# A ViT layer with a mixture of experts: the mixture's 192 inputs cut as 128 and 64, and a subtraction moved to GpSimd

## The chip, the cores and the metric

The kernel runs on one NeuronCore of a Trainium2 chip. The core has TensorE (PE in the rows; its weight loads are PEld), VectorE (DVE), ScalarE (ACT), GpSimd (POOL) and SyncE (SP, here only a queue of transfers). The metric is the device time of one execution in microseconds.

## The reference

64 images of 3 x 224 x 224 become 14 x 14 patches each. A linear layer makes 192 numbers of every patch, and with a class token there are 197 tokens an image. Then come two residual steps:

```python
h = h + attention(layernorm(h))     # 12 heads of 16, q and k normalised per head
h = h + ffn(layernorm(h))           # the mixture
# ffn, for each token x of 192:
scores = sigmoid(x @ gate_weight.T)             # 8 experts in 4 groups of 2
# 2 groups by scores + bias, in them 2 experts; weights = scores, normalised
h1 = einsum('td,eid->tei', x, w1); h3 = einsum('td,eid->tei', x, w3)   # 128 inner units
y = einsum('tei,edi,te->td', silu(h1) * h3, w2, cw)
z = silu(x @ sw1.T) * (x @ sw3.T) @ sw2.T       # a shared expert
return y + z
```

All is float32 at the interface.

## The kernel before

There are a setup and two stages, each with one instruction stream per engine, which meet at semaphores.

**Split numbers.** A float32 factor is held as two float16 tiles, hi (rounded, scaled) and lo (the rest). A product of two such factors is three products on TensorE: hi by hi, hi by lo, lo by hi, added up in PSUM. 192 inputs don't fit 128 rows of the array, so they are cut into two chunks of `KC` = 96 rows (index `k`). A 192-deep product is then 2 x 3 passes.

**Setup** (L184 to L231). SyncE loads all weights and constants, ScalarE writes each `hi` (L199), VectorE each `lo` (L217). The stage ends when all engines have ended.

**Attention stage** (`phase_a`). Its `run` goes over the images with a pipeline of five steps. The first 8 images are written out, then a hardware loop takes 8 images a turn (seven turns), then come five steps that empty the pipeline. Scores (L413) are products of 32-row pieces: four heads lie at rows 0, 32, 64 and 96, and their results in four PSUM banks. Each image's result goes to DRAM by SyncE (L319, L321).

**Mixture stage** (`phase_b`). The 12608 tokens are taken in 24 groups of 512 and a last one of 320, four tokens to a partition. Three groups and the last four are written out, the others go through a loop of two groups a turn. All nine experts (the shared one is number 8) are computed for all tokens, and the unchosen ones get weight 0. For each group and expert e:

- `inner_products` (PE): 12 passes of N = 512 into two banks, `ps_h1` and `ps_h3`, two of each, L905 (hi by hi), L907, L908. It waits until the multiplication two experts back is done.
- `silu` (ACT, L971): `act1` from `ps_h1`.
- `multiply` (DVE, L1098): `inner` = `ps_h3` times `act1`. Three `inner` buffers, so it also waits for the `inlo_done` of three experts back.
- `inner_first` (ACT, L979): `in_hi`, the float16 of `inner`.
- `inner_rest` (DVE, L1104): `in_lo` = `inner` - `in_hi`.
- `outer_products` (PE, L923 to L925): 12 passes of 192 columns into two banks `ps_y`. It waits for `in_lo`, and per half for the accumulation of the expert before.
- `accumulate` (DVE, L1122; L1128 for the shared expert): adds `ps_y`, weighted, to `acc`.

The order on each engine is fixed by hand. PE in step e runs inner(e) and then outer(e-2), after step 3 the next group's transposes (L878), after step 5 its gate (L890 to L892). DVE in step e runs multiply(e), inner_rest(e-1), accumulate(e-2), and then in steps 0 and 1 the last two parts of this group's routing; for the next group, statistics in step 1 (L1004, L1008), the normalisation `bnorm` in step 2 (L1017), `yT_lo` in step 4 (L1025) and the first three routing parts in steps 6 to 8. GpSimd has only `rstds`: after the statistics an addition (L1177) and a power (L1179) give `brstd`, for which `normalise` waits. The transposes turn `bnorm` into two chunks in `ps_x`, of which ACT (L955) makes `yT_hi` and DVE `yT_lo`. SyncE loads `hin` two groups ahead and stores `acc`.

Of the kernel before, what the change touches and what calls it, by code (L numbers as in the profile page):

```python
# [103 lines left out]
def vit_layer(nc, xp, w_lin, bias_cls, w_qkv, w_proj, w_gate, gate_bias, w13, w2,  # L104
              ident, before4, before8, out):
    hidden_dram = nc.dram_tensor("hidden_dram", [IMAGES, TOKENS, C], F32).ap()
    with ExitStack() as ctx:
# [7 lines left out]
        with ExitStack():  # L115
# [8 lines left out]
            gate_hi, gate_lo = split_pair("gate", [KC, 2, EXPERTS])  # L124
            w13_hi, w13_lo = split_pair("w13", [KC, 2, NE, 2, INTER])
# [13 lines left out]
            gate_f = stage("gate_f", [KC, 2, EXPERTS])  # L139
            w13_f = stage("w13_f", [KC, 2, NE, 2, INTER])  # L140
# [98 lines left out]
def phase_a(nc, xp, hidden_dram, sem, bufs):  # L239
# [510 lines left out]
def phase_b(nc, hidden_dram, out, sem, sb, bufs):  # L750
# [6 lines left out]
    with ExitStack() as ctx:  # L757
# [111 lines left out]
        def _(pe):  # L869
            def transposes(g):  # L870
                R = rows_of(g)
                pe.wait_ge(bnorm_done, g.times(1, 1))

                if reached(g.times(1)):
                    pe.wait_ge(tanh_done, g.times(1))
                for k in range(2):
                    for t in range(T):
                        last = pe.transpose(ps_x[k][0:KC, t * R:(t + 1) * R], bnorm[0:R, t, k * KC:(k + 1) * KC],  # L878
                                            id32[0:R, 0:R])
                last.then_inc(yT_done, 1)  # L880

            def gate(g):
# [3 lines left out]
                for t in range(T):  # L886
                    s = slice(t * R, (t + 1) * R)
                    dst = ps_x[0][0:R, t * E:(t + 1) * E]
                    for k in range(2):
# [4 lines left out]

            def inner_products(g, e):
# [7 lines left out]
                for w, bank in ((0, ps_h1[b]), (1, ps_h3[b])):  # L903
                    for k in range(2):
# [92 lines left out]
        def _(dve):  # L997
# [12 lines left out]
            def normalise(g):  # L1010
# [5 lines left out]
                for t in range(T):  # L1016
                    last = dve.tensor_scalar(bnorm[0:R, t, :], hin[p][0:R, t, :], bmv[0:R, t, 0:1],  # L1017
# [83 lines left out]
            def inner_rest(g, e):  # L1101
                N, b = T * rows_of(g), e % 3
                dve.wait_ge(inhi_done, g.times(NE, e + 1))
                dve.tensor_tensor(in_lo[b][:, 0:N], inner[b][:, 0:N], in_hi[b][:, 0:N],  # L1104
                                  ALU.subtract).then_inc(inlo_done, 1)

# [33 lines left out]
            def body(g):  # L1140
                following = g.back(-1)
                for e in range(NE):
                    multiply(g, e)
                    if e > 0:
                        inner_rest(g, e - 1)
                    elif g.back(1).active():
                        inner_rest(g.back(1), NE - 1)
# [87 lines left out]
```

## Time and profile before

| | us |
|---|---|
| runs shown, median (lowest to highest, 3 runs) | 2127.14 (2127.05 to 2127.79) |
| the profiled execution, its own time | 2126.83 |
| its span, first to last instruction | 2124.9 |
| PE busy | 1922.6 (90%) |
| PE weight loads busy | 1351.2 (64%) |
| DVE busy | 1320.9 (62%) |
| ACT busy | 908.2 (43%) |
| POOL busy | 42.2 (2%) |
| mean granted TensorE clock | 0.984 |

Busy times overlap between engines, and matmuls are pipelined, so that each one's length is longer than its distance from the next. The attention stage reaches to about 1186 us, the mixture stage from there to the end. A share of busy time over the whole span mixes these two stages.

### The profile page before, as it was taken

How to read it: one execution, taken by the hardware profiler on the slowest of the kernel's cores; microseconds unless marked ns; L12 is line 12 of the kernel's file. 1: busy time of each engine (PE TensorE's matmuls, PEld its weight loads, DVE VectorE, ACT ScalarE, POOL GpSimd, SP SyncE). 2: the span in 40 equal slices, each digit the busy share in tenths (PEclk: the TensorE clock that was granted, in tenths of full speed). 3: DMA queues.
4: the chain of work that ended last, by engine and by line, in shares of the span. 5: the costliest groups of instructions: out<-in, count | busy, mean ns of one | idle time of the engine just before them, and what ended most of it. 6: DMA issues, size and time to landing. Idle time of an engine off the chain costs nothing. (4 is left out here: it accounts for less than half of the span.)

```text
span 2124.9 us, 48134 instructions
## 1 busy us (share of the span) xinstructions
PE 1922.6 (90%) x17848; PEld 1351.2 (64%) x17848; DVE 1320.9 (62%) x3554; ACT 908.2 (43%) x1878; POOL 42.2 (2%) x63
## 2 busy tenths in 40 slices
PE   3999989899899898998998699999999999999998
PEld 3777767677677776776776355555555555555556
DVE  3444444444344444444444488788888888888888
ACT  2555545455455555555555233333333333333332
POOL 0000000000000000000000000000000000000000
PEclk9999999999999999999999799999999999999999
DMA  4011111111111111111110000000000000000000
GB/s 146 16 45 44 48 43 45 46 44 45 46 45 44 46 44 46 45 45 46 44 44 10 32 16 30 17 21 23 15 30 15 22 22 15 30 15 30 16 21 13
DMA packets 31517, 74.83 MB, mean 35 GB/s; under 512 B 3435, under 2 KB 16366, under 8 KB 31214
## 3 DMA queue, kind: packets, MB, share of 16 engines
q1 hardware_dynamic: 31310, 72.10, 10.8%
q8 instruction: 126, 2.06, 0.4%
q14 instruction: 81, 0.66, 0.1%
HBM read 52.73 MB, written 19.37 MB: 34 GB/s over the span
## 5 line engine op out<-in xcount | busy, mean ns | idle before, releaser
L571 ACT ACTIVATE prob<-ps_sc 99x792 f32<-99x792 f32 x384 | 317.5, 827 | 256.0 <-PE ps_sc L413 256.0
L357 PE MATMUL ps_hid<-lin_f,xin 128*99 128x192 f32 x1536 | 289.9, 333 | 65.7 <-DVE v L684 36.1
L905 PE MATMUL ps_h<-yT_hi,w_hi 96*128 96x512 f16 (+1 forms) x900 | 342.8, 381 | 0.0
L907 PE MATMUL ps_h<-yT_lo,w_hi 96*128 96x512 f16 (+1 forms) x900 | 341.3, 379 | 0.0
L908 PE MATMUL ps_h<-yT_hi,w_lo 96*128 96x512 f16 (+1 forms) x900 | 340.9, 379 | 0.0
L357 PEld LDWEIGHTS ps_hid<-lin_f,xin 128*99 128x99 f32 x1536 | 240.3, 169 | 77.0 <-issue 47.2
L979 ACT ACTIVATE in_hi<-inner 128x512 f16<-128x512 f32 (+1 forms) x225 | 140.3, 624 | 338.3 <-DVE inner L1098 338.3
L923 PE MATMUL ps_y<-w_hi,in_hi 128*128 128x192 f16 (+1 forms) x900 | 222.4, 247 | 40.6 <-DVE acc L1122 29.0
L971 ACT ACTIVATE act<-ps_h 128x512 f32<-128x512 f32 (+1 forms) x225 | 132.3, 588 | 278.6 <-PE ps_h L908 277.9
L1122 DVE SCALAR_TENSOR_TENSOR acc<-ps_y,comb,acc 128x192 f32<-128x192 f32 (+1 forms) x700 | 242.3, 407 | 0.0
L1098 DVE SCALAR_TENSOR_TENSOR inner<-ps_h,act 128x512 f32<-128x512 f32 (+1 forms) x225 | 152.7, 679 | 130.0 <-ACT act L971 119.8
L925 PE MATMUL ps_y<-w_hi,in_lo 128*128 128x192 f16 (+1 forms) x900 | 221.2, 246 | 0.0
L924 PE MATMUL ps_y<-w_lo,in_hi 128*128 128x192 f16 (+1 forms) x900 | 221.0, 246 | 0.0
L413 PE MATMUL ps_sc<-qT,kT 32*99 32x198 f32 x3072 | 178.4, 346 | 22.1 <-issue 16.4
L428 PE MATMUL ps_o<-prob,v 98*32 98x198 f32 (+1 forms) x3072 | 171.2, 341 | 0.8 <-ACT prob L571 0.8
L908 PEld LDWEIGHTS ps_h<-yT_hi,w_lo 96*128 96x128 f16 x900 | 88.3, 98 | 106.7 <-issue 4.9
L413 PEld LDWEIGHTS ps_sc<-qT,kT 32*99 32x99 f32 x3072 | 115.4, 160 | 60.1 <-issue 36.6
L1104 DVE TENSOR_TENSOR in_lo<-inner,in_hi 128x512 f16<-128x512 f32 (+1 forms) x225 | 151.3, 672 | 0.0
L657 DVE TENSOR_REDUCE qk_var<-qk_sq 99x24 f32<-99x384 f32 x128 | 70.3, 549 | 122.8 <-ACT qk_sq L530 122.8
L923 PEld LDWEIGHTS ps_y<-w_hi,in_hi 128*128 128x128 f16 (+1 forms) x900 | 88.1, 98 | 91.4 <-DVE acc L1122 34.7
L690 DVE RECIPROCAL o_rden<-ps_mix 99x12 f32<-99x12 f32 x128 | 29.7, 232 | 187.0 <-PE ps_mix L443 159.1
L907 PEld LDWEIGHTS ps_h<-yT_lo,w_hi 96*128 96x128 f16 x900 | 89.0, 99 | 80.3 <-issue 3.2
(112 smaller groups left out, 3050.1 us busy)
## 6 DMA issues: line engine op xcount, KB each, us to landing
xin<-xp SPq DMA_DIRECT2D x64, 594.0 KB, 3.9
hidden_dram<-h SPq DMA_DIRECT2D x64, 147.0 KB
hin<-hidden_dram SPq DMA_DIRECT2D x24, 384.0 KB, 3.0
out<-acc SPq DMA_DIRECT2D x24, 384.0 KB, 2.3
w_f<-w SPq DMA_DIRECT2D x1, 1728.0 KB, 11.5
hidden_dram<-h SPq DMA_DIRECT2D x64, 0.8 KB
w_f<-w SPq DMA_DIRECT2D x1, 864.0 KB, 13.0
lin_f<-w_lin SPq DMA_DIRECT2D x1, 576.0 KB
```

The costliest lines, as they stand in the source:

```text
L357: last = pe.matmul(hid[:, t, :], xin[q][:, k, t * TR:(t + 1) * TR], lin_f[:, k, :], start=(k == 0), stop=(k == PCHUNKS - 1))
L413: last = pe.matmul(sc[:, place, m, :], kT[p][rows, quad, m * TR:(m + 1) * TR], qT[p][rows, quad, :], start=True, stop=True)
L428: last = pe.matmul(o_quad[VB * place:VB * place + VB, :], v[p][rows, m, QUAD * quad + place, :], prob[quad][rows, place, m, :], start=(m = ...
L571: act.activation(prob[quad][:, places].rearrange("p h m s -> p h (m s)"), ps_sc[0:TR, places, 0:2 * SLOTS], ACT.Exp, scale=D ** -0.5 / (SQ ...
L905: pe.matmul(bank[:, 0:N], w13_hi[:, k, e, w, :], yT_hi[p][:, k, 0:N], start=(k == 0), stop=False)
L907: pe.matmul(bank[:, 0:N], w13_hi[:, k, e, w, :], yT_lo[p][:, k, 0:N], start=False, stop=False)
L908: last = pe.matmul(bank[:, 0:N], w13_lo[:, k, e, w, :], yT_hi[p][:, k, 0:N], start=False, stop=(k == 1))
L923: pe.matmul(dst, in_hi[b][:, s], w2_hi[:, e, :], start=True, stop=False)
L924: pe.matmul(dst, in_hi[b][:, s], w2_lo[:, e, :], start=False, stop=False)
L925: last = pe.matmul(dst, in_lo[b][:, s], w2_hi[:, e, :], start=False, stop=True)
L1098: dve.scalar_tensor_tensor(out=inner[e % 3][:, 0:N], in0=ps_h3[b][:, 0:N], scalar=SA / SS, in1=act1[b][:, 0:N], op0=ALU.mult, op1=ALU.mult ...
L1122: last = dve.scalar_tensor_tensor(out=acc[p][0:R, t, :], in0=ps_y[half_no][0:R, u * C:(u + 1) * C], scalar=comb[p][0:R, t, e:e + 1], in1=b ...
```

## The change

The mixture's and the gate's input is cut as 128 and 64 instead of 96 and 96. The 64 stand twice in the rows of the second chunk: `bnorm` is 256 wide, its last 64 columns the columns 128 to 191 again, so that the transposes give 128 rows in both chunks. The weights are laid out to match by the host (`tailed`). In the second chunk of `w13_hi` rows 0 to 63 are hi and rows 64 to 127 lo of the same weights, so that one pass with `yT_hi` gives two of the three products. The third, hi by `yT_lo`, is a product of 64 rows; for w1 its weights lie in rows 0 to 63 of `w13_lo`, for w3 in rows 64 to 127, and the two are issued one after the other into different banks. `inner_rest` moves from DVE to GpSimd, where `rstds` comes before the one of expert 1. In the attention stage 16 images are written out instead of 8.

```diff
 (setup, VectorE: for w13)
+dve.scalar_tensor_tensor(out=lo[:, 0], in0=f[:, 0], scalar=SW, in1=hi[:, 0], ...)
+dve.tensor_copy(lo[0:64, 1, :, 0, :], hi[0:64, 1, :, 0, :])
+dve.tensor_copy(lo[64:128, 1, :, 1, :], hi[64:128, 1, :, 1, :]).then_inc(w_tail_done, 1)
+dve.wait_ge(w_tail_done, 1)
+dve.scalar_tensor_tensor(out=hi[64:128, 1], in0=f[64:128, 1], scalar=SW, in1=hi[64:128, 1], ...)
 (attention stage, run)
-            first = 1
+            first = 2
 (PE, transposes)
-                for k in range(2):
-                    for t in range(T):
-                        last = pe.transpose(ps_x[k][0:KC, t * R:(t + 1) * R], bnorm[0:R, t, k * KC:(k + 1) * KC],
+                for t in range(T):
+                    s = slice(t * R, (t + 1) * R)
+                    for k in range(2):
+                        last = pe.transpose(ps_x[k][:, s], bnorm[0:R, t, k * 128:(k + 1) * 128], id32[0:R, 0:R])
 (PE, gate: five products a token tile in place of six)
+                    pe.matmul(dst, yT_hi[p][:, 0, s], gate_hi[:, 0], start=True, stop=False)
+                    pe.matmul(dst, yT_hi[p][:, 0, s], gate_lo[:, 0], start=False, stop=False)
+                    pe.matmul(dst, yT_lo[p][:, 0, s], gate_hi[:, 0], start=False, stop=False)
+                    pe.matmul(dst, yT_hi[p][:, 1, s], gate_hi[:, 1], start=False, stop=False)
+                    last = pe.matmul(dst, yT_lo[p][:, 1, s], gate_lo[:, 1], start=False, stop=True)
 (PE, inner_products)
-                for w, bank in ((0, ps_h1[b]), (1, ps_h3[b])):
-                    for k in range(2):
-                        pe.matmul(bank[:, 0:N], w13_hi[:, k, e, w, :], yT_hi[p][:, k, 0:N],
-                                  start=(k == 0), stop=False)
-                        pe.matmul(bank[:, 0:N], w13_hi[:, k, e, w, :], yT_lo[p][:, k, 0:N], start=False, stop=False)
-                        last = pe.matmul(bank[:, 0:N], w13_lo[:, k, e, w, :], yT_hi[p][:, k, 0:N],
-                                         start=False, stop=(k == 1))
+                for w, bank in enumerate(banks):
+                    pe.matmul(bank, w13_hi[:, 0, e, w, :], y_hi[:, 0], start=True, stop=False)
+                    pe.matmul(bank, w13_hi[:, 0, e, w, :], y_lo[:, 0], start=False, stop=False)
+                    pe.matmul(bank, w13_lo[:, 0, e, w, :], y_hi[:, 0], start=False, stop=False)
+                    pe.matmul(bank, w13_hi[:, 1, e, w, :], y_hi[:, 1], start=False, stop=False)
+                for w, bank in enumerate(banks):
+                    rows = slice(64 * w, 64 * w + 64)
+                    last = pe.matmul(bank, w13_lo[rows, 1, e, w, :], y_lo[rows, 1], start=False, stop=True)
 (DVE, normalise, for each of four t)
-                    last = dve.tensor_scalar(bnorm[0:R, t, :], hin[p][0:R, t, :], bmv[0:R, t, 0:1],
+                    dve.tensor_scalar(bnorm[0:R, t, 0:C], hin[p][0:R, t, :], bmv[0:R, t, 0:1],
+                                      brstd[0:R, t:t + 1], ALU.subtract, ALU.mult)
+                    last = dve.tensor_scalar(bnorm[0:R, t, C:256], hin[p][0:R, t, 128:C], bmv[0:R, t, 0:1],
                                              brstd[0:R, t:t + 1], ALU.subtract, ALU.mult)
 (inner_rest and its calls are gone from DVE)
 (GpSimd)
+            def inner_rest(g, e):
+                N, b = T * rows_of(g), e % 3
+                pool.wait_ge(inhi_done, g.times(NE, e + 1))
+                settle(pool, settled)
+                pool.tensor_tensor(in_lo[b][:, 0:N], inner[b][:, 0:N], in_hi[b][:, 0:N],
+                                   ALU.subtract).then_inc(inlo_done, 1)
             def body(g):
-                if g.back(-1).active():
-                    rstds(g.back(-1))
+                for e in range(NE):
+                    if e == 1 and g.back(-1).active():
+                        rstds(g.back(-1))
+                    inner_rest(g, e)
```

## Rows read from the trace of the kernel before

**Rows 1.** The page, section 2: busy tenths in 40 slices of the span.
```profile
PE   3999989899899898998998699999999999999998
...
DVE  3444444444344444444444488788888888888888
```

**Rows 2.** Stretches of the mixture stage: start:end us, length, busy us (instructions), TensorE clock.
```profile
2036.20:2072.40 36.20, 34.47 (x252) 20.53 (x251) 31.20 (x89) 11.99 (x22) 1.79 (x2) 1.00 0.03 12
...
1420.65:1458.30 37.65, 35.61 (x247) 21.05 (x245) 30.68 (x87) 12.09 (x21) 1.26 (x2) 0.95 0.06 21
```

**Rows 3.** Timeline of one expert: start us, us, engine, line, what [idle before].
```profile
1603.49 0.38 PE L905 MATMUL ps_h<-yT_hi,w_hi 96*128 96x512 f16 x1
...
1606.08 0.25 PE L923 MATMUL ps_y<-w_hi,in_hi 128*128 128x192 f16 x1
...
1606.91 0.69 DVE L1098 SCALAR_TENSOR_TENSOR inner<-ps_h,act 128x512 f32<-128x512 f32 x1 [0.47 <-ACT act L971]
...
1607.07 0.38 PE L905 MATMUL ps_h<-yT_hi,w_hi 96*128 96x512 f16 x1
...
1607.52 0.68 DVE L1104 TENSOR_TENSOR in_lo<-inner,in_hi 128x512 f16<-128x512 f32 x1
1607.71 0.63 ACT L979 ACTIVATE in_hi<-inner 128x512 f16<-128x512 f32 x1 [0.84 <-DVE inner L1098]
...
1608.12 1.39 DVE L1122 SCALAR_TENSOR_TENSOR acc<-ps_y,comb,acc 128x192 f32<-128x192 f32 x4
```

**Rows 4.** Timeline of VectorE alone, one group: four of its L1098.
```profile
1660.88 0.69 DVE L1098 SCALAR_TENSOR_TENSOR inner<-ps_h,act 128x512 f32<-128x512 f32 x1
...
1669.02 0.69 DVE L1098 SCALAR_TENSOR_TENSOR inner<-ps_h,act 128x512 f32<-128x512 f32 x1 [1.89 <-ACT act L971]
...
1684.39 0.69 DVE L1098 SCALAR_TENSOR_TENSOR inner<-ps_h,act 128x512 f32<-128x512 f32 x1 [0.20 <-DVE rank L1059]
...
1697.87 0.66 DVE L1098 SCALAR_TENSOR_TENSOR inner<-ps_h,act 128x512 f32<-128x512 f32 x1
```

**Rows 5.** Timeline around the normalisation of the group that begins in rows 4.
```profile
1661.40 1.04 POOL L1179 TENSOR_TENSOR brstd<-bvareps,minus_half 128x4 f32<-128x4 f32 x1
...
1663.39 1.24 DVE L1017 TENSOR_SCALAR bnorm<-hin,bmv,brstd 128x192 f32<-128x192 f32 x4
...
1664.69 1.08 PE L878 MATMUL ps_x<-id,bnorm 128*96 128x128 f32 x8 [0.49 <-DVE bnorm L1017]
...
1665.60 0.38 PE L905 MATMUL ps_h<-yT_hi,w_hi 96*128 96x512 f16 x1
```

**Rows 6.** Timeline of the attention stage where 32-row score products begin and end.
```profile
1154.80 0.25 PE L342 MATMUL ps_mix<-proj_hi,onT_lo 96*99 96x192 f16 x1
...
1154.97 0.93 PE L413 MATMUL ps_sc<-qT,kT 32*99 32x198 f32 x16
...
1155.83 0.88 PE L428 MATMUL ps_o<-prob,v 98*32 98x198 f32 x16
```

**Rows 7.** The page, section 5: the score products by line and shape, whole span.
```profile
L413 PE MATMUL ps_sc<-qT,kT 32*99 32x198 f32 x3072 | 178.4, 346 | 22.1 <-issue 16.4
```

**Rows 8.** Groups of GpSimd alone, by shape, whole span.
```profile
L1179 POOL TENSOR_TENSOR brstd<-bvareps,minus_half 128x4 f32<-128x4 f32 x24 | 31.7, 1321 | 2.0
L1177 POOL TENSOR_SCALAR bvareps<-bmv 128x4 f32<-128x4 f32 x24 | 5.5, 228 | 1990.7 <-DVE bmv L1008 1990.7
...
L226 POOL MEMSET qk_norm<- 99x768 f32 x2 | 1.4, 737 | 0.0
```

**Rows 9.** SyncE's timeline of image stores, on both sides of one loop edge.
```profile
263.72 0.34 SPq L319 DMA_DIRECT2D hidden_dram<-h  x1
...
287.67 0.33 SPq L319 DMA_DIRECT2D hidden_dram<-h  x1
...
305.02 0.34 SPq L319 DMA_DIRECT2D hidden_dram<-h  x1
```

**Rows 10.** Timeline of the setup: VectorE's last conversion of weights.
```profile
17.75 6.82 DVE L217 SCALAR_TENSOR_TENSOR w_lo<-w_f,w_hi 96x4608 f16<-96x4608 f32 x2 [6.01 <-ACT w_hi L199]
```

More of the change, by code:

```diff
@@ L123, in vit_layer @@
             proj_hi, proj_lo = split_pair("proj", [KC, 2, C])
-            gate_hi, gate_lo = split_pair("gate", [KC, 2, EXPERTS])
-            w13_hi, w13_lo = split_pair("w13", [KC, 2, NE, 2, INTER])
+            gate_hi, gate_lo = split_pair("gate", [128, 2, EXPERTS])
+            w13_hi, w13_lo = split_pair("w13", [128, 2, NE, 2, INTER])
             w2_hi, w2_lo = split_pair("w2", [INTER, NE, C])
@@ L138, in vit_layer @@
             proj_f = stage("proj_f", [KC, 2, C])
-            gate_f = stage("gate_f", [KC, 2, EXPERTS])
-            w13_f = stage("w13_f", [KC, 2, NE, 2, INTER])
+            gate_f = stage("gate_f", [128, 2, EXPERTS])
+            w13_f = stage("w13_f", [128, 2, NE, 2, INTER])
             w2_f = stage("w2_f", [INTER, NE, C])
@@ L767, in phase_b @@
         brstd = sb("brstd", [128, T])
-        bnorm = sb("bnorm", [128, T, C])
-        yT_hi = [sb(f"yT_hi{p}", [KC, 2, GT], F16) for p in range(2)]
-        yT_lo = [sb(f"yT_lo{p}", [KC, 2, GT], F16) for p in range(2)]
+        bnorm = sb("bnorm", [128, T, 256])
+        yT_hi = [sb(f"yT_hi{p}", [128, 2, GT], F16) for p in range(2)]
+        yT_lo = [sb(f"yT_lo{p}", [128, 2, GT], F16) for p in range(2)]
         act1 = [sb(f"act1{p}", [INTER, GT]) for p in range(2)]
@@ L902, in inner_products @@
                     pe.wait_ge(mul_done, g.times(NE, e - 1))
-                for w, bank in ((0, ps_h1[b]), (1, ps_h3[b])):
-                    for k in range(2):
-                        pe.matmul(bank[:, 0:N], w13_hi[:, k, e, w, :], yT_hi[p][:, k, 0:N],
-                                  start=(k == 0), stop=False)
-                        pe.matmul(bank[:, 0:N], w13_hi[:, k, e, w, :], yT_lo[p][:, k, 0:N], start=False, stop=False)
-                        last = pe.matmul(bank[:, 0:N], w13_lo[:, k, e, w, :], yT_hi[p][:, k, 0:N],
-                                         start=False, stop=(k == 1))
+                banks = (ps_h1[b][:, 0:N], ps_h3[b][:, 0:N])
+                y_hi, y_lo = yT_hi[p][:, :, 0:N], yT_lo[p][:, :, 0:N]
+                for w, bank in enumerate(banks):
[6 more added lines that the diff above has]
+                    last = pe.matmul(bank, w13_lo[rows, 1, e, w, :], y_lo[rows, 1], start=False, stop=True)
                 last.then_inc(inner_done, 1)
@@ L1024, in yT_out @@
                     dve.wait_ge(yThi_done, g.times(2, k + 1))
-                    dve.scalar_tensor_tensor(out=yT_lo[p][:, k, 0:N], in0=ps_x[k][0:KC, 0:N], scalar=SX,
+                    dve.scalar_tensor_tensor(out=yT_lo[p][:, k, 0:N], in0=ps_x[k][:, 0:N], scalar=SX,
                                              in1=yT_hi[p][:, k, 0:N], op0=ALU.mult,
@@ L1099, in multiply @@
                                          in1=act1[b][:, 0:N], op0=ALU.mult, op1=ALU.mult).then_inc(mul_done, 1)
[L1101 to L1105, printed above, removed]
             def accumulate(g, e):
@@ L1143, in body @@
                     multiply(g, e)
[L1144 to L1147, printed above, removed]
                     if e > 1:
@@ L1213 @@
     w2 = np.concatenate([np.asarray(L0_ffn_w2), np.asarray(L0_ffn_sw2)[None]])
-    w13 = np.stack([w1, w3], 1).reshape(NE, 2, INTER, 2, KC).transpose(4, 3, 0, 1, 2)
+    w13 = tailed(np.stack([w1, w3], 1).reshape(NE * 2 * INTER, C)).reshape(128, 2, NE, 2, INTER)
     gate_bias = np.empty((128, LANES, EXPERTS), np.float32)
```

33 lines of the change are left out of this document (24 added, 9 removed).

## The prediction

> **What bounds the kernel now.** I read the page's slices first. From slice 23 on, the mixture stage, PE reads 9 and VectorE (DVE) 8 in nearly every slice [rows 1]. Two engines are almost full, and a cut on one alone would soon meet the other. The stretches of one group's length say the same: of 36.20 us in the unrolled tail PE is busy 34.47 and DVE 31.20. In the loop 17 stretches of 37.65 follow each other, and five of them read a clock of 0.95, which is about 3.8 us at 1.2 GHz instead of 2.4 in each [rows 2].
>
> Then one expert in order of time. PE takes 2.59 us for the twelve inner products (1603.49 to 1606.08, 0.2155 each) and 0.99 for the outer ones, 3.58 together. The multiplication on DVE starts 3.42 us after the first inner product (2.59 plus 0.83 of pipeline end and Silu). On DVE inner, in_lo and the four acc follow 0.61, 0.60 and 1.30 us apart, 2.51 in all [rows 3]. DVE has more to do in some experts: routing in 0, 1, 6, 7, 8, statistics in 1, normalisation in 2, yT_lo in 4. Write D2 for the start of expert 2's multiplication. DVE's starts are D2 = 1660.88, D4 = 8.14 later, D8 another 15.37 later, and the next D2 13.48 after that, 36.99 in all [rows 4]. So who sets the end changes within a group:
> - D8 to D2: three steps of 4.49 against PE's 3.58. DVE binds, and PE waits for acc.
> - D2 to D4: a chain. Normalisation (starts D2+2.51, takes 1.24), transposes on PE, inner products of expert 4 from D2+4.72 [rows 5], then 3.42 to D4. 4.72 + 3.42 = 8.14.
> - D4 to D8: four PE steps of 3.58 plus the gate and a little of DVE, 15.37. PE binds.
>
> **The change, part by part.**
>
> *Nine passes.* Per expert eight 128-row products and two 64-row ones on different rows and banks. If the two run side by side, that is 9 x 0.2155 = 1.94 us. The attention stage shows that they can: 16 passes on 32-row pieces take 0.93 us, of which the last one's own length is 0.35 [rows 7], so 0.04 apart where a 192-column f16 pass alone has 0.08. It also shows what the change of piece costs. L342 to the first L413 is 0.17 us against the usual 0.08, so 0.09 going in. Coming out, the last L413 starts near 1155.55 and L428 at 1155.83; 0.28 less 0.155 for its share of four is 0.12 [rows 6]. I take 0.21 for both, so I = 2.15 us an expert. The bounds: 1.94 (both hidden) and 2.40 (no overlap, ten passes, 2.155, plus 0.24).
>
> The Trainium skill speaks against this part (TensorEngine Tiling (Array Packing), Key Properties): going from one tiling to another, not merely to another tile, drains TensorE. The gaps at L413 agree in direction. The page gives no price, so the sum keeps the rows' 0.21; with nothing for it, it would be rival 1's.
>
> *inner_rest from DVE to GpSimd.* On its new engine it issues a wait, a semaphore increment and the subtraction, no DMA; nothing of SyncE's queue is passed. It takes 0.60 us of DVE per expert [rows 3]. No GpSimd subtraction of 128x512 is in the trace. Its memset of 768 elements takes 0.737 and a 4-element operation 0.228 [rows 8], so a stream costs about 0.83 ns an element. One stream of 512 gives 0.65 us, two (both inputs one after the other) 1.08, three 1.51. I take 1.15, next to two; the lower bound is 0.5, and for the upper one I double it to 2.4. The Trainium skill (GPSIMD Engine Reference, section 3.1) has 4497 ns for a two-input add of 2048 elements, some 1.1 us for 512 by proportion; the sum is the same by it.
>
> Usually this hides. in_hi starts 0.80 after inner and takes 0.63 [rows 3], so in_lo would be there about D+2.8, and PE asks for it two inner products later, D+4.5 or more. The exception is expert 1. GpSimd now runs rstds before inner_rest(1), and rstds waits for DVE's statistics, which end at D2. The power starts at D2+0.52 and takes 1.04 in this group [rows 5], 1.32 in the mean [rows 8]: it ends at D2+1.84. Then 0.1 of wait, 1.15 of subtraction and 0.1 to PE: outer products of expert 1 at D2+3.2. Behind that wait on PE stand the outer products (0.99), the transposes, and inner(4). The transposes take 0.91 now [rows 5]; with 128 columns in place of 96 I take 1.1. PE reaches inner(4) at D2 + 3.2 + 0.99 + 1.1 = 5.3, against 4.72 now.
>
> *Normalisation.* Four more DVE operations of 64 columns. The present four take 1.16 from start to start, 0.29 each; at a third of the width I take 0.15, so 0.6 us (bounds 0.3, 1.16). DVE then finishes at D2+3.7, before the outer products of expert 1 end at 4.19, so GpSimd's delay covers it. Without that delay it is what is late: D2+3.85 for the transposes.
>
> *One group after.* D2 to D4: 5.3 + 2.15 + 0.83 = 8.3 (was 8.14). D4 to D8: 15.37 less 4 x 0.44 for PE, less 0.1 for the gate's four fewer products and 0.1 for DVE's in expert 7: 13.4. D8 to D2: DVE loses 3 x 0.60, 13.48 - 1.80 = 11.7. Sum 33.4, which is 3.6 less. For 24 full groups: -86 us. The last group of 320 columns, smaller and with no next group: -2. The first normalisation stands free: +0.6.
>
> *TensorE's clock.* Now PE stands in pieces of about 1 us around experts 1 to 3. Afterwards it has inner(3) done near D2+0.2 and waits to D2+3.2, in one piece. Five of 17 stretches now lose about 1.9 us of PE time [rows 2], though part of that falls where PE waits anyway. I expect half of the 24 groups to gain such an episode at 1.2 us: +14 (bounds 0 and +35).
>
> *Attention, loop from image 16.* Stores lie 17.35 us apart, at the loop edge 23.95 [rows 9]. There are six such edges, and they cost between 2.8 and 6.6 us more, 27.4 together. The first images, unrolled, run at the same 17.3. One edge goes: -4.6.
>
> *Setup.* The stage ends with DVE's conversions, 6.82 us for 6336 elements, 1.08 ns each [rows 10]. After: the same elements, two copies of 1152 (0.6 to 2.5 us), a wait in between, and w13's transfer a third larger ahead of them. I take +3.5 (0.6 to 6.3). Gate pieces are too small to count.
>
> **Sum.** The profiled execution took 2126.83 us (span 2124.9 and 1.9 around it), 0.3 under the median of 2127.14, so no correction. 2126.8 - 86 - 2 + 0.6 + 14 - 4.6 + 3.5 = 2052 us.
>
> **Rivals.**
> 1. *The 64-row pair costs nothing beyond its pass.* I = 1.94: expert 4 comes 0.21 earlier, D4 to D8 0.7 shorter (DVE's routing in 7 takes a little back). Group 32.4, 1.0 less in each of 24: 2052 - 24 = 2028, and 2014 if the clock doesn't fall more often. For it: loads of weights run ahead of the products everywhere in this trace. Against: the gaps at L413 [rows 6].
> 2. *The pair runs as two passes, or draining costs more.* I = 2.40, group 34.6: 2052 + 30 = 2082. For it: no 64-row piece is in the trace. Together with a subtraction of 2 us, 2102.
> 3. *It ends on the other side: GpSimd becomes the bound.* With P for one subtraction a group needs 9 P + 1.6 us there (the power and its addition, [rows 8]), and no work of another engine can pass it, since outer products and, three experts on, the multiplication wait for in_lo. The loop's groups now take 36.99 [rows 4] to 37.65, about 37.3, which it equals at P = 3.97. At P = 4.5 a group takes 42.1, 24 x 4.8 = +115: 2240 us. For it: a power of 4 elements takes 1.32 us there, so its time there isn't set by width alone. Against: the memset's rate, from which 3.97 is more than twice three streams.
> 4. *DVE doesn't get shorter*, because GpSimd's traffic slows its operations by what it was relieved of. A power takes 1.04 us in one group and 1.32 in the mean [rows 5, 8], so something is shared beside DVE's work. D8 to D2 then stays 13.48: +43, 2095.
>
> **Chances and range.** The forecast with its own terms (2035 to 2070) 0.45; rival 1 0.22; rival 2 0.15; rival 3 0.06; rival 4 0.07; a mixture that is 0.2% or less from before 0.02; the rest below 2010, 0.03. The range 2010 to 2100 holds the first cases. About 0.2% (4 us) is what a measurement can tell from no change. Faster by more 0.91, same 0.02, slower 0.07 (rival 3 and a sliver of 4).
>
> **What would show it.** Inner products of one expert span 2.15 us from the first to the outer products' first, 1.94 by rival 1, 2.4 by rival 2. GpSimd's subtractions read near 1.15 us, busy about 290 us in total. Steps from D8 to D2 shrink to 11.7. The longest PE wait in each group ends with GpSimd's in_lo ahead of expert 1's outer products, about 3 us. The clock reads 0.95 in more than half of the stretches. Five loop edges are left in the attention stage and the image distance stays 17.35. The forecast is wrong if groups stay above 36 us, or if PE waits for in_lo in experts other than 1.

## The result, and the profile after

The changed kernel takes 2147.07 us (median of 4 runs, 2145.86 to 2147.82) against 2127.1: ratio 1.0096, interval 1.008 to 1.0112. The forecast was 2052 us with a range from 2010 to 2100. It is slower where faster was forecast. The profiled span is 2146.0 us, 21.1 longer than before, and its granted clock 0.957 instead of 0.984.

The page's slices, which answer [rows 1], show PE and DVE both lower than before in the mixture stage, and GpSimd (POOL) at 2 to 3. Neither of the two is nearly full any more.

```profile
PE   3999999899899998998998688888888798897888
...
DVE  3444444444444444444443587887878878788787
...
POOL 0000000000000000000000123333233322333332
```

Two stretches of the mixture stage (start:end, length, then busy us of PE, weight loads, DVE, ACT and POOL with instructions, the TensorE clock, DMA share, GB/s), against [rows 2]: PE is busy 31 to 32 us where it was 35.6, at a clock of 0.91 and 0.95.

```profile
1383.00:1420.65 37.65, 31.37 (x219) 17.80 (x218) 29.23 (x79) 11.25 (x20) 10.91 (x11) 0.91 0.06 21
1600.00:1638.33 38.33, 32.05 (x226) 17.87 (x225) 30.61 (x83) 11.88 (x21) 11.61 (x11) 0.95 0.06 21
```

The inner products of one expert [rows 3], from its first to the first outer product: 2.14 us (1605.59 to 1607.73), forecast 2.15. The two 64-row products run as a pair, one row for both. The distances from start to start on its two sides are 0.31 and 0.32 against the usual 0.2155; together that is the price of the piece change, 0.20.

```profile
1605.59 0.38 PE L929 MATMUL ps_h<-yT_hi,w_hi 128*128 128x512 f16 x1
...
1607.41 0.10 PEld L936 LDWEIGHTS ps_h<-yT_lo,w_lo 64*128 64x128 f16 x2 [0.42 <-issue]
...
1607.73 0.26 PE L950 MATMUL ps_y<-w_hi,in_hi 128*128 128x192 f16 x1
```

VectorE's four multiplications of one group [rows 4]. D4, D8, D2 and the next D4 here: D4 to D8 14.18, D8 to D2 13.15, D2 to D4 10.91 (forecast 13.4, 11.7, 8.3).

```profile
1605.33 0.69 DVE L1127 SCALAR_TENSOR_TENSOR inner<-ps_h,act 128x512 f32<-128x512 f32 x1 [4.14 <-ACT act L998]
...
1619.51 0.69 DVE L1127 SCALAR_TENSOR_TENSOR inner<-ps_h,act 128x512 f32<-128x512 f32 x1 [0.20 <-DVE rank L1088]
...
1632.66 0.68 DVE L1127 SCALAR_TENSOR_TENSOR inner<-ps_h,act 128x512 f32<-128x512 f32 x1
...
1643.57 0.69 DVE L1127 SCALAR_TENSOR_TENSOR inner<-ps_h,act 128x512 f32<-128x512 f32 x1 [3.53 <-ACT act L998]
```

Around that group's normalisation [rows 5], D2 = 1632.66. PE waits for GpSimd's in_lo(1) until 1635.55, D2+2.9 (forecast 3.2). But the normalisation, which began at D2+1.9, is over only near D2+5.4, and PE starts inner(4) at D2+7.4 instead of 5.3. Look at two rows: a 192-column operation of DVE of 0.98 us, where the next one takes 0.37, and a 64-column one of 1.15, where the others take 0.30. They end 0.05 to 0.12 us after GpSimd's two subtractions do. And the first products of expert 4 read 0.63 us each instead of 0.38: TensorE is at 1.2 GHz.

```profile
1633.26 1.04 POOL L1197 TENSOR_TENSOR brstd<-bvareps,minus_half 128x4 f32<-128x4 f32 x1
...
1634.26 2.28 POOL L1203 TENSOR_TENSOR in_lo<-inner,in_hi 128x512 f16<-128x512 f32 x2
1634.56 0.98 DVE L1044 TENSOR_SCALAR bnorm<-hin,bmv,brstd 128x192 f32<-128x192 f32 x1
...
1635.45 1.15 DVE L1046 TENSOR_SCALAR bnorm<-hin,bmv,brstd 128x64 f32<-128x64 f32 x1
...
1635.55 0.25 PE L950 MATMUL ps_y<-w_hi,in_hi 128*128 128x192 f16 x1 [2.54 <-POOL in_lo L1203]
...
1636.52 0.37 DVE L1044 TENSOR_SCALAR bnorm<-hin,bmv,brstd 128x192 f32<-128x192 f32 x1
...
1638.27 1.96 PE L901 MATMUL ps_x<-id,bnorm 128*128 128x128 f32 x8 [1.56 <-DVE bnorm L1046]
...
1640.03 0.63 PE L929 MATMUL ps_h<-yT_hi,w_hi 128*128 128x512 f16 x1
```

By shape over the mixture stage (line, engine, operation, names, shapes, count, busy us, mean ns, idle before), first after, then before:

```profile
L1044 DVE TENSOR_SCALAR bnorm<-hin,bmv,brstd 128x192 f32<-128x192 f32 x92 | 48.1, 523 | 0.0
L1046 DVE TENSOR_SCALAR bnorm<-hin,bmv,brstd 128x64 f32<-128x64 f32 x92 | 47.1, 512 | 0.0
...
L1079 DVE TENSOR_TENSOR cmp<-masked 128x256 f32<-128x256 f32 x24 | 26.3, 1095 | 0.0
...
L1079 DVE TENSOR_TENSOR cmp<-gsum 128x64 f32<-128x64 f32 x24 | 20.9, 869 | 0.0
L1093 DVE TENSOR_SCALAR score<-half 128x32 f32<-128x32 f32 x24 | 20.7, 861 | 1.1 <-ACT half L989 1.1
L1100 DVE TENSOR_SCALAR chosen<-rank 128x16 f32<-128x16 f32 x24 | 20.2, 841 | 0.0
```

```profile
L1017 DVE TENSOR_SCALAR bnorm<-hin,bmv,brstd 128x192 f32<-128x192 f32 x92 | 28.5, 372 | 0.0
...
L1050 DVE TENSOR_TENSOR cmp<-masked 128x256 f32<-128x256 f32 x24 | 9.9, 414 | 0.0
...
L1050 DVE TENSOR_TENSOR cmp<-gsum 128x64 f32<-128x64 f32 x24 | 5.1, 214 | 0.0
...
L1064 DVE TENSOR_SCALAR score<-half 128x32 f32<-128x32 f32 x24 | 4.1, 171 | 1.2 <-ACT half L962 1.2
...
L1071 DVE TENSOR_SCALAR chosen<-rank 128x16 f32<-128x16 f32 x24 | 3.9, 163 | 0.0
```

So the chosen, score and comparison operations (parts of the routing) got 0.66 to 0.69 us longer each with the same operands; inner (687 ns) and acc (407 ns), one input of which is in PSUM, did not change by a nanosecond. GpSimd's side [rows 8]: a subtraction takes 1.159 us, forecast 1.15.

```profile
L1203 POOL TENSOR_TENSOR in_lo<-inner,in_hi 128x512 f16<-128x512 f32 x211 | 243.5, 1159 | 473.7 <-ACT in_hi L1006 473.7
L1197 POOL TENSOR_TENSOR brstd<-bvareps,minus_half 128x4 f32<-128x4 f32 x23 | 23.9, 1037 | 1.9
```

The rest of the forecast: the stores of images, the first and the last [rows 9], and the setup's conversions [rows 10]. Five loop edges are left of six, as forecast (24.05, 20.36, 22.16, 24.03, 21.93 us).

```profile
93.17 0.37 SPq L341 DMA_DIRECT2D hidden_dram<-h  x1
...
1185.78 0.32 SPq L341 DMA_DIRECT2D hidden_dram<-h  x1
```

```profile
21.93 1.96 DVE L239 SCALAR_TENSOR_TENSOR w_lo<-w_f,w_hi 128x1728 f16<-128x1728 f32 x1
```

The last store was at 1185.49 before, so everything ahead of the mixture stage cost +0.3 us (forecast -1.1). The conversions end at 23.9, earlier than the 24.6 of before [rows 10]. The loss is all in the mixture stage.

Below, "group" is the mean distance from one group's D2 to the next over groups 3 to 21. The three parts are means that leave out the first of these, so they don't always add up to it. "Low clock" is the number and total length of the episodes at 1.2 GHz that begin between 1206 us (about where the mixture's first multiplication stands) and 2130 us. The one that is left in e6 and in e8 to e13 begins behind the last multiplication.

| kernel | us | ratio to before [interval] | group | D2-D4 | D4-D8 | D8-D2 | low clock |
|---|---|---|---|---|---|---|---|
| before | 2127.1 | | 37.32 | 8.71 | 15.37 | 13.30 | 7, 22 us |
| after | 2147.1 | 1.0096 [1.008, 1.0112] | 38.33 | 11.23 | 14.19 | 12.95 | 24, 133 us |
| e1_vector | 2129.6 | 1.0018 [1.0006, 1.0029] | 37.54 | 9.90 | 14.47 | 13.26 | 15, 82 us |
| e2_only_pool | 2143.4 | 1.0085 [1.0067, 1.0103] | 37.63 | 9.32 | 15.30 | 12.89 | 11, 44 us |
| e3_rstds_later | 2143.7 | 1.0084 [1.0061, 1.0106] | 38.30 | 10.57 | 14.20 | 13.60 | 24, 120 us |
| e4_fill | 2103.5 | 0.9892 [0.9874, 0.991] | 36.47 | 9.38 | 14.19 | 12.95 | 2, 7 us |
| e5_probe | 2207.8 | 1.0371 [1.0348, 1.0394] | 40.94 | 13.10 | 14.53 | 13.35 | 23, 154 us |
| e6_before_fill | 2120.0 | 0.9965 [0.9952, 0.9979] | 36.80 | 8.16 | 15.37 | 13.30 | 1, 4 us |
| e7_tail_scalar | 2087.3 | 0.9806 [0.9784, 0.9828] | 35.82 | 8.14 | 14.47 | 13.27 | 8, 27 us |
| e8_tail_fill | 2083.7 | 0.979 [0.9768, 0.9811] | 35.66 | 7.96 | 14.46 | 13.26 | 1, 1 us |
| e9_mixed | 2042.1 | 0.9593 [0.9577, 0.9609] | 33.85 | 8.07 | 13.12 | 12.68 | 1, 1 us |
| e10_three | 2073.5 | 0.9736 [0.972, 0.9752] | 35.14 | 8.07 | 13.81 | 13.29 | 1, 2 us |
| e11_pool_tail_fill | 2082.3 | 0.9785 [0.9768, 0.9802] | 35.59 | 8.49 | 14.24 | 12.91 | 1, 1 us |
| e12_order_only | 2082.2 | 0.9776 [0.9751, 0.9802] | 35.56 | 7.97 | 14.33 | 13.29 | 1, 3 us |
| e13_mixed_no_order | 2068.5 | 0.972 [0.9691, 0.9749] | 35.12 | 8.07 | 14.29 | 12.81 | 1, 2 us |

### The profile page after: what moved, and what is told of

It is laid out like the page before. It is cut to its first block and busy times, and to the rows that moved or that the text cites. A ratio compares the mean times of both kernels' runs of the same rounds, so it can differ in the third digit from the quotient of the medians.

```text
span 2146.0 us, 47266 instructions
## 1 busy us (share of the span) xinstructions
PE 1866.3 (87%) x17298; PEld 1298.9 (61%) x17298; DVE 1316.4 (61%) x3435; ACT 905.4 (42%) x1878; POOL 290.7 (14%) x288
## 5 line engine op out<-in xcount | busy, mean ns | idle before, releaser
L1203 POOL TENSOR_TENSOR in_lo<-inner,in_hi 128x512 f16<-128x512 f32 (+1 forms) x225 | 256.4, 1144 | 503.8 <-ACT in_hi L1006 503.8
L950 PE MATMUL ps_y<-w_hi,in_hi 128*128 128x192 f16 (+1 forms) x900 | 229.3, 255 | 106.5 <-POOL in_lo L1203 60.5
L951 PE MATMUL ps_y<-w_lo,in_hi 128*128 128x192 f16 (+1 forms) x900 | 226.9, 252 | 0.0
L952 PE MATMUL ps_y<-w_hi,in_lo 128*128 128x192 f16 (+1 forms) x900 | 226.8, 252 | 0.0
L1195 POOL TENSOR_SCALAR bvareps<-bmv 128x4 f32<-128x4 f32 (+1 forms) x25 | 5.7, 228 | 1343.4 <-DVE bmv L1035 1343.4
L929 PE MATMUL ps_h<-yT_hi,w_hi 128*128 128x512 f16 (+1 forms) x450 | 178.6, 397 | 0.0
L930 PE MATMUL ps_h<-yT_lo,w_hi 128*128 128x512 f16 (+1 forms) x450 | 177.7, 395 | 0.0
L931 PE MATMUL ps_h<-yT_hi,w_lo 128*128 128x512 f16 (+1 forms) x450 | 175.9, 391 | 0.0
L932 PE MATMUL ps_h<-yT_hi,w_hi 128*128 128x512 f16 (+1 forms) x450 | 174.3, 387 | 0.0
## 6 DMA issues: line engine op xcount, KB each, us to landing
w_f<-w SPq DMA_DIRECT2D x1, 864.0 KB, 11.3
```

The costliest lines, as they stand in the source:

```text
L929: pe.matmul(bank, w13_hi[:, 0, e, w, :], y_hi[:, 0], start=True, stop=False)
L930: pe.matmul(bank, w13_hi[:, 0, e, w, :], y_lo[:, 0], start=False, stop=False)
L931: pe.matmul(bank, w13_lo[:, 0, e, w, :], y_hi[:, 0], start=False, stop=False)
L932: pe.matmul(bank, w13_hi[:, 1, e, w, :], y_hi[:, 1], start=False, stop=False)
L950: pe.matmul(dst, in_hi[b][:, s], w2_hi[:, e, :], start=True, stop=False)
L951: pe.matmul(dst, in_hi[b][:, s], w2_lo[:, e, :], start=False, stop=False)
```

## The experiments

**e1 and e2: the two halves alone.** e1 is the changed kernel with in_lo back on VectorE; e2 is the kernel before with in_lo on GpSimd and nothing else.

```diff
# e1: after, the subtraction back on VectorE (e2: before, the same edit the other way).
# Shortened: the function and its calls move with the line.
-                pool.tensor_tensor(in_lo[b][:, 0:N], inner[b][:, 0:N], in_hi[b][:, 0:N],
+                dve.tensor_tensor(in_lo[b][:, 0:N], inner[b][:, 0:N], in_hi[b][:, 0:N],
                                   ALU.subtract).then_inc(inlo_done, 1)
```

> The kernel after the change with inner_rest put back on VectorE, in its old place; nine passes, 128/64 and the attention loop stay. Theory 1 (VectorE instructions that read or write SBUF through both ports wait for a running GpSimd subtraction): every long one of the kernel after (score 861 ns, chosen 841, first cmp 869 and 1095, bnorm 523 and 512) falls back to before's 171, 163, 214, 414, 372 and about 300; D8 to D2 13.1 to 13.5 us, D2 to D4 about 8.7, group about 35.5, 2080 us. Theory 2 (only the late in_lo of expert 1 and the lowered clock cost time): the same direction, but the long VectorE instructions should not change by this.

> The kernel before with inner_rest alone moved to GpSimd (96/96, twelve passes). Theory 1: VectorE gets back what it was relieved of (D8 to D2 stays near 13.1), D2 to D4 near 11.3 by the late in_lo of expert 1; group 39.6, 2182 us. Theory 2: D8 to D2 falls to 11.7, group 38.2, 2149 us.

Measured: 1.0018 and 1.0085. Moving in_lo to GpSimd alone makes the kernel 0.85% slower, and nine passes with their four 64-column operations give nothing. Both expectations missed in part. In e1 the long operations fell back as theory 1 had it, but the kernel came out at 2129.6 and not at 2080: the 64-column operations and the clock, which e7 and e8 price, weren't in it. e2's 2143 us is near theory 2's 2149, but not by its way: D8 to D2 is 12.89 and not 11.7, and D2 to D4 is 9.32 where theory 1 had 11.3. In e2 the same operations are longer as in after (score 861 ns, chosen 841, the 256-wide comparison 1095), with twelve passes and no 64-column operations there: it is GpSimd's subtraction that does it, not the new shapes.

What GpSimd did to VectorE's steps can be added up. Step e reaches from expert e's multiplication to the next one (means of the loop). The table takes DVE's steps in e1, subtracts the 0.60 of in_lo that goes, adds the extra time of that step's operations from the rows above (for the 64-column bnorm against e1's 306 ns), and compares with after:

| step | e1 | -0.60, plus the wait of | gives | after |
|---|---|---|---|---|
| 0 | 4.84 | comparison 128x256, 0.68 | 4.92 | 4.96 |
| 1 | 4.69 | none | 4.09 | 4.08 |
| 2 | 4.52 | four bnorm at 523 for 372 ns, four at 512 for 306, 1.43 | 5.35 | 5.39 |
| 6 | 3.32 | score, 0.69 | 3.41 | 3.43 |
| 7 | 3.83 | comparison 128x64, 0.66 | 3.89 | 3.95 |
| 8 | 3.75 | chosen, 0.68 | 3.83 | 3.90 |

Of 5.4 us that VectorE is relieved of in a group, 4.1 come back as waits. Steps 3 to 5 have few such operations: step 4 keeps the relief (3.71 to 3.15), step 5 doesn't change (3.61 to 3.65), and step 3 (5.37 to 5.84) is set by TensorE and its clock (3.98 in e4, where the clock is held).

**e3: GpSimd's order.** The one wait that I had forecast, rstds ahead of inner_rest(1), is taken away.

```diff
-                    if e == 1 and g.back(-1).active():
+                    if e == 2 and g.back(-1).active():
                         rstds(g.back(-1))
```

> The kernel after with one line changed: rstds stands before inner_rest(2) instead of before inner_rest(1), so no subtraction waits behind the statistics. Theory 2: the wait of about 2.5 us before expert 1's outer products goes, the clock stays up, group 34.3, about 2065 us. Theory 1: that wait goes too, but D8 to D2 stays at 13.1 or more and bnorm still collides; group about 36, 2090 to 2100 us.

Measured: 2143.7; the interval of its ratio holds after's 1.0096, and both theories had expected a gain of about 50 us or more. D2-D4 loses 0.66 and D8-D2 gains 0.65: the wait moves. That it was long in after (24 waits, 60.5 us in all, below) doesn't make it worth anything.

```profile
PE ps_y L950 <- POOL in_lo L1203: 60.5, 24, 2.9
```

The trace of e3 shows where it moved to. Without the power ahead of it, the subtraction of expert 1 starts already in step 1. So one operation of the normalisation meets a subtraction where two did, but the routing in step 1 meets one too (4.08 to 4.73 us). There an operation on 4 columns takes 0.82 us, 0.17 in e1. The reduction ahead of it, with one input in SBUF as well, runs wholly beside the subtraction and keeps its 0.19 (means 187 and 186 ns in e3 and e1):

```profile
1586.55 1.16 POOL L1203 TENSOR_TENSOR in_lo<-inner,in_hi 128x512 f16<-128x512 f32 x1 [3.80 <-ACT in_hi L1006]
1586.69 0.19 DVE L1114 TENSOR_REDUCE den<-wsel 128x4 f32<-128x32 f32 x1
1586.91 0.82 DVE L1115 TENSOR_SCALAR den<-den 128x4 f32<-128x4 f32 x1
```

**e4: the clock.** Eleven idle products of 512 columns, whose result nobody reads, fill TensorE's wait in step 3.

```diff
+                    if e == 3 and following.active():
+                        p = g.mod(2)
+                        for _ in range(11):
+                            pe.matmul(ps_x[1][:], w13_hi[:, 0, e, 0, :], yT_hi[p][:, 0, :], start=True, stop=True)
```

> The kernel after with 11 idle products of 512 columns (2.4 us) on TensorE between inner products and outer products of expert 3, into a bank that nobody reads then; they fill the wait for in_lo, so only the clock can change. If the half clock after that wait is on the path (6.8 us of it per group in 13 of 24): clock near 1.0 in the mixture stage and 2 us a group less, 2100 us. If it is not: 2147 within 5 us.

Measured: 2103.5, 43.6 us less than after, with 2 episodes at 1.2 GHz instead of 24. D4-D8 and D8-D2 are the same to 0.01, D2-D4 is 1.85 shorter. D2 to D4 in a group of after, then in one of e4: 10.91 at 0.84, 9.34 at 1.00.

```profile
1632.66:1643.57 10.91, 6.80 (x42) 4.38 (x42) 7.38 (x21) 3.43 (x6) 4.67 (x5) 0.84 0.12 36
```

```profile
1572.64:1581.98 9.34, 7.79 (x53) 4.42 (x53) 7.38 (x20) 3.31 (x6) 4.68 (x5) 1.00 0.13 42
```

So idle work makes the kernel faster, because it stands where TensorE waits anyway and what follows then runs at 2.4 GHz.

**e5: a probe.** e1, with one more GpSimd subtraction per expert on buffers of its own. No engine waits for its result.

```diff
+                for e in range(NE):
...
+                    pool.wait_ge(inhi_done, g.times(NE, e + 1))
...
+                    pool.tensor_tensor(probe[:, 0:N], probe_in[:, 0:N], probe_in[:, 0:N], ALU.subtract).then_inc(probed, 1)
```

> e1_vector (inner_rest on VectorE) with an extra GpSimd subtraction of 128x512 on tiles of its own, at the moments at which the kernel after runs its own; nobody waits for it. So only a shared resource can slow the rest. Theory 1 (VectorE's instructions with both SBUF ports wait for it): score, chosen, the first cmp and the first bnorm grow by 0.5 to 0.8 us each as in the kernel after, D8 to D2 grows by 1.3 us or more over e1_vector's 13.26, D2 to D4 by about 1; 3 us a group, about 2200 us. Theory 2 (it was waits and order): e1_vector's 2130 us within 5.

Measured: 1.0371, 78 us more than e1. GpSimd and then VectorE in the same time (start, us): each DVE operation of 192 columns that begins beside a probe ends 0.11 after it does and takes 1.09; the next free one takes 0.37.

```profile
1666.84 1.07 POOL L1225 TENSOR_TENSOR probe<-probe_in 128x512 f16<-128x512 f32 x1 [0.17 <-issue]
1668.08 1.07 POOL L1225 TENSOR_TENSOR probe<-probe_in 128x512 f16<-128x512 f32 x1 [0.17 <-POOL probe L1225]
```

```profile
1666.93 1.09 DVE L1047 TENSOR_SCALAR bnorm<-hin,bmv,brstd 128x192 f32<-128x192 f32 x1
...
1668.17 1.09 DVE L1047 TENSOR_SCALAR bnorm<-hin,bmv,brstd 128x192 f32<-128x192 f32 x1
...
1669.41 0.37 DVE L1047 TENSOR_SCALAR bnorm<-hin,bmv,brstd 128x192 f32<-128x192 f32 x1
```

In the mean bnorm at 192 columns is 835 ns in place of 372. This rules out a wait for data: the probe shares none with the kernel. Its 78 us aren't all such waits: low-clock time rose from 82 to 154 us too. Of the 3.4 us that it adds to a group, 3.2 lie in D2 to D4. The 1.3 expected in D8 to D2 didn't come (13.26 to 13.35): there score and the 64-wide comparison begin only when a probe is about to end, and read 0.20 and 0.24.

**e6: before, with idle products** (4 in step 2, 3 in step 3 of the kernel before).

> The kernel before with idle products of 512 columns in two of TensorE's waits of each group: 4 ahead of the outer products in step 2, 3 ahead of the transposes. It prices the clock in the kernel before, so that the filled kernels are compared with a filled one. Groups without a fall of the clock take 36.66 us and the others about 38.6 (mean 37.32): all at 36.7, -16 us, 2111. If the idle products themselves delay the outer products: 2125 or more.

Measured: 2120.0, not the 2111 expected (group 36.80). The kernel before had 7 us to gain from its clock.

**e7 and e8: the 64-column copies.** e7 is e1 with the four extra DVE operations replaced by one copy on ScalarE, and the transposes in the order of columns; e8 adds 4 + 5 idle products.

```diff
-                    last = dve.tensor_scalar(bnorm[0:R, t, C:256], hin[p][0:R, t, 128:C], bmv[0:R, t, 0:1], ...
+                act.activation(bnorm[0:R, :, C:256], bnorm[0:R, :, 128:C], ACT.Copy).then_inc(tail_done, 1)
```

> e1_vector with the 64 repeated columns written by one ScalarE copy a group in place of four VectorE instructions. VectorE's step 2 falls from 4.52 to about 3.65 us, as before the change. If the clock theory holds (less work on TensorE, more falls of the clock) most of it is given back: 2115 to 2128 us. If the repeated columns themselves were what ate the nine passes' gain: 0.9 us a group, 2108 us or less with the clock as in e1_vector.

> e7_tail_scalar with idle products: 4 ahead of the outer products in step 2, 5 ahead of the transposes. Clock theory: no falls, every group near 35.6 us, 1.9 under e1_vector's mean of 37.54: 2083 us. Without the clock's part: as e7_tail_scalar.

Measured: 2087.3 and 2083.7. The copies cost 1.7 us a group in e1 (37.54 to 35.82): 0.89 in step 2 (4.52 to 3.63), 0.86 in step 3 (5.37 to 4.51). The second part is clock: low-clock time falls from 82 to 27 us, and between e4 and e11, which differ by the same copies with the clock held, step 2 changes by 0.90 and step 3 by 0.01. e7 came out 21 us below the 2108 of its expectation, which left the clock as in e1. e8 against e6, both with the clock held: 36.80 to 35.66, so nine passes are worth 1.1 a group while VectorE keeps in_lo.

**e9, e10, e11: GpSimd again, with e8's clock.** e9 gives GpSimd experts 3 to 8 and moves the routing ahead of the accumulation in steps 6 to 8; e10 gives it experts 3 to 5, unmoved; e11 all nine (after, with ScalarE's copy and 11 idle products).

```diff
# e9
+        ON_POOL = [3, 4, 5, 6, 7, 8]
+                    if following.active() and e > 5:
+                        route(following, e - 6)
                     if e > 1:
                         accumulate(g, e - 2)
...
-                        if e > 5:
-                            route(following, e - 6)
```

> e8 with GpSimd doing the subtraction in_lo for experts 3 to 8 again and VectorE for 0 to 2, and with the routing of steps 6 to 8 moved ahead of the accumulation, so that its comparisons of two SBUF inputs run before the GpSimd subtraction starts. The tail copy on ScalarE and the idle products stay. Theory A (two-SBUF-input operations of VectorE wait for a GpSimd subtraction that runs beside them, and order can avoid it): D8 to D2 shrinks from 13.26 by up to two or three subtractions of 0.6, a group takes 33.6 to 34.5 instead of 35.66, about 2035 to 2055 us. Theory B (whatever is taken from VectorE is given back somewhere): group 35.5 or more, 2080 us or more, ratio to before 0.978 or above.

> e8 with GpSimd doing in_lo for experts 3, 4 and 5 alone, where VectorE has little but PSUM-source and tensor-by-tensor multiplications to do; nothing reordered. Theory A: few operations of VectorE meet a subtraction, its steps 4 to 6 become shorter by up to 0.6 where VectorE sets them; but TensorE sets most of D4 to D8 (14.46), so a group gains 0.2 to 0.6, 2070 to 2079 us. Theory B: D4 to D8 does not move or grows, 2084 us or more.

> The changed kernel with all nine subtractions on GpSimd, but with the 64-column copy as one ScalarE operation (no extra VectorE normalisations) and 11 idle products in step 3, so that the clock stays up. Against e8 (2083.7, all subtractions on VectorE) it gives what GpSimd relief is worth with nothing else different, against e4 (2103.5) what the four extra normalisations cost. Theory A (relief and port waits cancel nearly, waits somewhat larger in steps 1 and 2): 2078 to 2095 us, group 35.4 to 36.1, with the four full-width normalisations at 0.5 us each in place of 0.37 and the 128x256 comparison at 1.1 in place of 0.41. If the ports had no part and only the clock had spoilt the forecast: 33.5 to 34 a group, 2030 to 2045 us.

Measured: 2042.1, 2073.5 and 2082.3. e11 is the same as e8 (their intervals overlap): all nine subtractions on GpSimd are worth nothing against none, with the clock at 0.988 in both. e10 gains 0.5 a group, in D4-D8 (14.46 to 13.81). e9 is 42 us below e8 and 85 below before.

**e12 and e13: e9's two edits apart.** e12 is e8 with the moved routing alone; e13 is e9 with the routing unmoved.

> The control to e9: e8 with routing moved ahead of the accumulation in steps 6 to 8, but all subtractions on VectorE, none on GpSimd. If e9's gain is GpSimd's relief made usable by the order (theory A), the order alone changes little: a group stays within 0.3 of 35.66, 2077 to 2090 us. If the order itself had brought e9's gain (theory C: routing's results were simply late), this one reaches e9: 2040 to 2055 us.

> e9 with the routing behind the accumulation again, where the changed kernel has it; GpSimd still does in_lo for experts 3 to 8. Theory A: the 128x256 comparison, score and chosen meet the subtraction again and read 0.8 to 1.1 us in place of 0.41 and 0.17, some 0.6 us in each of steps 6, 7 and 8, so a group is 1.2 to 2.0 longer than e9's 33.85, about 2070 to 2090 us, and e8's relief is used up. Theory C' (it is which experts GpSimd takes that matters, not the order): those operations stay at 0.41 and 0.17 and the group within 0.3 of e9's, about 2042 to 2049 us.

Measured: groups of 35.56 and 35.12, where e8 has 35.66 and e9 33.85. Order alone gives 0.1, the choice of experts 0.5, both 1.8. The groups of e13, then of e9:

```profile
L1111 DVE TENSOR_TENSOR cmp<-gsum 128x64 f32<-128x64 f32 x23 | 21.2, 920 | 0.0
L1125 DVE TENSOR_SCALAR score<-half 128x32 f32<-128x32 f32 x23 | 20.2, 878 | 0.0
L1132 DVE TENSOR_SCALAR chosen<-rank 128x16 f32<-128x16 f32 x23 | 20.0, 869 | 0.0
```

```profile
L1111 DVE TENSOR_TENSOR cmp<-gsum 128x64 f32<-128x64 f32 x24 | 5.2, 215 | 0.0
...
L1132 DVE TENSOR_SCALAR chosen<-rank 128x16 f32<-128x16 f32 x24 | 4.0, 166 | 0.0
L1125 DVE TENSOR_SCALAR score<-half 128x32 f32<-128x32 f32 x23 | 3.9, 171 | 0.0
```

In e9 score, chosen and comparison start right behind inner, while GpSimd still waits for in_hi; when its subtraction starts, VectorE is in the four acc, which it leaves alone. In the whole of e9 and e10 no tensor_tensor or tensor_scalar without a PSUM input begins during a subtraction. e13 came out 1.5 us under its expected 2070 to 2090: theory A's waits came back, but they didn't use up all of the relief, since it is still 15 us below e8.

## Why the prediction was wrong

- **Where the ends are, D2, D4, D8:** held but for experts 6 and 7. D4 to D8 was forecast as TensorE's own time; in after VectorE ends steps 6 and 7, with its waits (D8 in the answer to [rows 4] follows right behind VectorE's own rank). I = 2.15 held (2.14), and so did the subtraction of 1.15 (1.159) and the outer products of expert 1 at D2+3.2 (2.9). Rivals 1, 2 and 3 are out. The 1.15 was in part luck: 0.83 ns an element doesn't follow from the two rows it was taken from. They give (0.737 - 0.228) / 764 = 0.67 ns, and so 0.57, 0.91 and 1.25 us for one, two and three streams, with 1.15 between the last two.
- **"D8 to D2: DVE loses 3 x 0.60, 13.48 - 1.80 = 11.7": the step that failed.** It priced the waits of VectorE's other operations beside the moved subtraction at nothing. D8 to D2 went from 13.30 to 12.95 in the mean. The relief came, and two waits of 0.68 took most of it back. The same mistake is in D4 to D8: 13.4 forecast, 14.19 measured, with waits of 0.69 and 0.66 in steps 6 and 7; e9, which has no waits there, measures 13.12. This is rival 4, which I gave 0.07 and priced at +43 for D8 to D2 alone. I had no reason against it, and I had its sign in [rows 5, 8], a GpSimd power of 1.04 us in one group and 1.32 in the mean. I called it "something shared" and didn't look for what. Two rows of the kernel before, one group on, would have told: the power begins 0.01 after VectorE's in_lo and takes 1.56, where in [rows 5] it begins 0.09 before it and takes 1.04.

```profile
1698.45 0.68 DVE L1104 TENSOR_TENSOR in_lo<-inner,in_hi 128x512 f16<-128x512 f32 x1
1698.46 1.56 POOL L1179 TENSOR_TENSOR brstd<-bvareps,minus_half 128x4 f32<-128x4 f32 x1
```

The Trainium skill says it outright (SBUF — State Buffer, section Who interferes with whom): a VectorE instruction with two SBUF inputs, or one in a two-port mode, contends with a GpSimd instruction that reads SBUF, and whoever comes first keeps the port to its end. For the subtractions the trace agrees; GpSimd's power of four elements is an exception (last section). In after, GpSimd's subtraction, a comparison of two SBUF inputs that begins in it, and the one behind that:

```profile
1617.17 1.16 POOL L1203 TENSOR_TENSOR in_lo<-inner,in_hi 128x512 f16<-128x512 f32 x1 [2.28 <-ACT in_hi L1006]
...
1617.46 0.94 DVE L1079 TENSOR_TENSOR cmp<-gsum 128x64 f32<-128x64 f32 x1
...
1618.33 0.21 DVE L1080 TENSOR_TENSOR eq<-gsum 128x64 f32<-128x64 f32 x1
```

- **"GpSimd's delay covers it" (normalisation):** failed. The four 64-column operations take 0.23 us each from start to start, 0.9 together and not 0.6, and two of the eight operations wait for a subtraction. It ends at D2+5.4, not D2+3.7, so it is what is late, and the forecast wait for in_lo(1) was the one that is hidden (e3). Of D2 to D4, 11.23 less the forecast 8.3: clock 1.85 (e4), copies 0.89 (e4 9.38 to e11 8.49), the rest 0.2.
- **Clock, +14 with bounds 0 and +35:** 44 (e4), outside my bounds. The mechanism was named rightly, a single long piece of waiting per group, and the term was mis-sized: an episode came in every group (24), not in half, and cost 1.85 us each time, not 1.2.
- **Setup +3.5, edge -4.6:** +0.3 together at the last store, forecast -1.1. Among the kernels with this setup the last store lies between 1181.0 (e1) and 1189.2 (e5), so the parts aren't resolved.

The sum of the errors in a loop group: D2 to D4 2.9, of which 0.6 stood in the forecast as the clock's 14 us; D4 to D8 0.8; D8 to D2 1.25; together 4.35, 104 us over 24 groups. The time was missed by 95; the unrolled groups at both ends are a little shorter (36.9 at the start, 36.7 and 37.4 near the end).

Nine passes and relief do both pay where the waits are gone (e8 against e6, e9 against e12). That e9's 2042 us lies 10 below the forecast of 2052 confirms nothing: e9 leaves three of nine subtractions on VectorE, has ScalarE's copy and has its clock held, and the forecast has none of these.

Open: why bnorm, score, chosen and den (tensor_scalar, one SBUF tensor input) wait as the comparisons with two do, while a reduction with one input doesn't (e3). Size isn't it, since 4 columns wait as 192 do. By the Trainium skill (same section) it would be tensor_scalar's two-port mode; no run here varied their type.

## What to carry to other kernels

Before moving work from VectorE to GpSimd, list the VectorE operations that run beside it and have no input in PSUM. Here nearly every tensor_tensor and tensor_scalar of this kind that began during a GpSimd subtraction of 512 columns waited for its end (in after 146 of 148); the reductions didn't. Order the first ahead of it, and put PSUM-reading work and reductions beside it; then the relief is real. When TensorE gets less to do and one long wait in place of several short ones, read its granted clock first, and price what follows the wait at 1.2 GHz.

## What the hardware did that was not expected

- The wait goes both ways, but it isn't always one for the whole instruction. GpSimd's power of four elements takes 1.037 us in after, where VectorE runs only acc beside it, 1.321 before, and 1.573 in e9, where it starts with VectorE's in_lo. The kernel before has two kinds of groups: in 14 in_lo begins 0.01 to 0.02 before the power, which then takes 1.56; in 10 it begins 0.08 to 0.35 after it, and both keep their usual times, 1.04 and 0.68. A two-input operation that begins inside the power doesn't wait for its end, as it would for a subtraction's. e9's rows:

```profile
L1246 POOL TENSOR_TENSOR in_lo<-inner,in_hi 128x512 f16<-128x512 f32 x144 | 166.7, 1158 | 354.8 <-ACT in_hi L1037 354.8
L1240 POOL TENSOR_TENSOR brstd<-bvareps,minus_half 128x4 f32<-128x4 f32 x23 | 36.2, 1573 | 1.9
```

- Idle products in a wait shortened the whole by 43.6 us (e4) and even the kernel before by 7 (e6).
- A 64-column operation of VectorE takes 0.23 us from start to start where a 192-column one takes 0.29: a third of the width is four fifths of the time.
